# A graph network on one core: the segment mask as loaded bytes, and the sum of messages on TensorE

## The reference

```python
h = (x @ W).reshape(n, H, C)
# loops are added: every node is its own neighbour too
e = leaky_relu(a_src[src] + a_dst[dst], 0.2)
e = exp(e - segment_max(e, dst)[dst])
alpha = e / (segment_sum(e, dst)[dst] + 1e-16)
msg = h[src] * alpha[:, :, None]
out = segment_sum(msg, dst) + bias
f = gelu(out)
f = (f - mean(f)) / sqrt(var(f) + 1e-5) * gamma + beta
return f + x
```

## Time and profile before

| | us |
|---|---|
| median of three runs | 3763.0 (3749.06 to 3767.47) |
| the profiled execution | 3756.52 |
| its span, first to last instruction | 3754.8 |
| VectorE busy | 3277.5 (87%) |
| TensorE busy | 2538.7 (68%) |
| ScalarE busy | 2505.5 (67%) |
| GpSimd busy | 2442.9 (65%) |
| mean granted TensorE clock | 0.782 of full |

### The profile page before, as it was taken

One profiled execution on the slowest core, in us unless ns is written; L12 is line 12 of the kernel. 1 busy time (PEld: TensorE's weight loads), 2 busy tenths in 40 slices (PEclk: granted clock), 3 DMA queues, 4 the chain that ended last, 5 costly groups with the idle time before them and its releaser, 6 DMA issues. The chain is left out here.

```text
span 3754.8 us, 45520 instructions
## 1 busy us (share of the span) xinstructions
PE 2538.7 (68%) x10538; PEld 1633.2 (43%) x10538; DVE 3277.5 (87%) x7566; ACT 2505.5 (67%) x5570; POOL 2442.9 (65%) x2202
## 2 busy tenths in 40 slices
PE   5888888888724444267567567658788885777774
PEld 3555555555401222166566556524444442444442
DVE  5999999999877999699789789869999996998886
ACT  3888888888832666556546557747777774665554
POOL 4666666666614666477677677667666633787777
PEclk9999999999966777576676677679998986665555
DMA  3888877777647999578778678623333323333331
GB/s 104 203 223 207 212 216 210 217 212 216 199 122 210 268 271 272 172 227 275 226 227 277 214 229 257 194 80 95 87 85 84 85 69 85 89 98 92 97 96 58
DMA packets 421065, 643.89 MB, mean 171 GB/s; under 512 B 128031, under 2 KB 226728, under 8 KB 420798
## 3 DMA queue, kind: packets, MB, share of 16 engines
q1 hardware_dynamic: 351038, 527.96, 46.8%
q0 software_dynamic: 69760, 113.02, 12.7%
HBM read 347.78 MB, written 296.81 MB: 172 GB/s over the span
## 5 line engine op out<-in xcount | busy, mean ns | idle before, releaser
L915 POOL DMA_INDIRECT gs_t<-table_x,slot_idx x392 | 439.5, 1121 | 310.8 <-POOLq L87 126.1
L1651 POOL DMA_INDIRECT gs_g<-table_h,slot_idx x392 | 417.7, 1066 | 158.4 <-issue 115.8
L522 POOL DMA_INDIRECT gs<-x,src_idx x200 | 220.6, 1103 | 261.3 <-DMA xd_rows<-gd 150.6
L1290 POOL DMA_INDIRECT slot_idx<-node_map,src_idx x200 | 250.7, 1253 | 192.0 <-DMA slot_idx<-node_map,src_idx 95.8
L385 PE MATMUL ps<-ident,gs_g 128*128 128x128 f32 x588 | 131.7, 366 | 264.0 <-DMA gs_g<-table_h,slot_idx 156.7
L1702 ACT ACTIVATE h_e_g<-zb_g,inv 128x128 f32<-128x128 f32 x392 | 124.9, 390 | 249.6 <-DVE zb_g L1785 249.6
L2008 POOL DMA_INDIRECT out<-x_t,end_idx x196 | 234.4, 1196 | 60.3 <-issue 59.7
L1651 POOL DMA_INDIRECT gs_g<-table_x,slot_idx x196 | 208.1, 1062 | 96.4 <-issue 94.9
L522 POOL DMA_INDIRECT gd<-x,dst_idx x200 | 223.3, 1116 | 60.9 <-issue 60.0
L915 POOL DMA_INDIRECT own_t<-table_x,own_idx x196 | 221.4, 1129 | 59.7 <-issue 59.7
L1770 DVE TENSOR_TENSOR_SCAN agg_g<-same_seg,agg_g,ps 128x512 f32<-128x512 uint8 x147 | 187.3, 1274 | 83.3 <-PE ps L385 83.2
(11 more groups left out here) (378 smaller groups left out, 9015.5 us busy)
## 6 DMA issues: line engine op xcount, KB each, us to landing
table_x<-x_b SPq DMA_DIRECT2D x99, 512.0 KB
table_h<-h_b SPq DMA_DIRECT2D x98, 512.0 KB
x_in<-x SPq DMA_DIRECT2D x49, 512.0 KB
table_h<-h_e_g SPq DMA_DIRECT2D x98, 256.0 KB
own_g<-table_h SPq DMA_DIRECT2D x98, 256.0 KB, 4.7
pen_t<-pen_row SPq DMA_DIRECT2D x98, 256.0 KB, 3.8
table_x<-x_b SPq DMA_DIRECT2D x48, 384.0 KB
y_g<-table_x SPq DMA_DIRECT2D x48, 384.0 KB, 6.2
```

Of the source, the lines that this page charges most:

```text
L522: pool.indirect_dma_start(out=to[k % 3][:, j * D:(j + 1) * D], out_offset=None, in_=x, in_offset=bass.IndirectOffsetOnAxis(ap=of[:, n:n + ...
L915: pool.indirect_dma_start(out=self.B[L % RING][g][:, t * D:(t + 1) * D], out_offset=None, in_=table, in_offset=bass.IndirectOffsetOnAxis(a ...
L1290: pool.indirect_dma_start(out=slot_idx[:, t:t + 1], out_offset=None, in_=node_map, in_offset=bass.IndirectOffsetOnAxis(ap=src_idx[:, t:t + ...
L1651: pool.indirect_dma_start(out=gs[c % 6][:, j * D:(j + 1) * D], out_offset=None, in_=tables[layer], in_offset=bass.IndirectOffsetOnAxis(ap= ...
```

## The change

- Preparation: VectorE copies the mask to bytes (`same_u8`), and SyncE stores it as `same_row`.
- Softmax part: SyncE loads `same_row` once, broadcast to 128 partitions, into `same_seg`; it waits for the landing at the end of the part.
- Stage 3: the loads of `nst` and ScalarE's casts are gone; the scan reads its mask from `same_seg`.
- Stage 3: `with_self` is gone from VectorE. TensorE multiplies the identity with the message total and with the own message, accumulating both in `T_D2` (signal `o_ps`), and Gelu reads `T_D2`. The own product of the next pair, which writes the same bank, waits for Gelu instead of the own message. In TensorE's order the four products stand between the source products and the own products. `as_b` is free for its next load after `o_ps`.

```diff
@@ -94,6 +94,7 @@
     nst_row = dram("nst_row", [1, ET])
     nxt_row = dram("nxt_row", [1, ET])
     cnt_row, own_row = dram("cnt_row", [1, ET]), dram("own_row", [1, ET])
+    same_row = dram("same_row", [1, ET], U8)
     z8, a8 = dram("z8", [8, ET]), dram("a8", [8, ET])
     xsT_d, xdT_d = dram("xsT_d", [P, ET]), dram("xdT_d", [P, ET])
     xd_rows = dram("xd_rows", [ET, D])
@@ -154,6 +155,7 @@
         edge_i = tb("edge_i", [H, 2, 4, P], I32)
         edge_f = tb("edge_f", [H, 2, 4, P])
         mark = tb("mark", [H, 2, 5, P])
+        same_u8 = tb("same_u8", [H, 2, P], U8)
         att = tb("att", [P, 2, D])
         prod = tb("prod", [P, 4, D])
         sums = tb("sums", [P, 6, 4])
@@ -202,7 +204,9 @@
                 sp.wait_ge(S("marks"), 2)
                 for row, k in ((nst_row, 1), (pen_row, 2), (nxt_row, 0)):
                     sp.dma_start(row.rearrange("o (h r c) -> (o r) h c", h=2, c=P), mark[:, :, k, :]).then_inc(S("rows_stored"), 16)
-                sp.wait_ge(S("rows_stored"), 48)
+                sp.wait_ge(S("same_u8"), 1)
+                sp.dma_start(same_row.rearrange("o (h r c) -> (o r) h c", h=2, c=P), same_u8[:]).then_inc(S("rows_stored"), 16)
+                sp.wait_ge(S("rows_stored"), 64)
                 sp.wait_ge(S("stored"), 32)
 
             @block.gpsimd
@@ -274,6 +278,7 @@
                 v.wait_ge(S("m"), 3)
                 V.tensor_tensor(mark[:, :, 3, :], mark[:, :, 4, :], edge_f[:, :, 1, :], ALU.add).then_inc(S("marks"), 1)
 
+                V.tensor_copy(same_u8[:], mark[:, :, 1, :]).then_inc(S("same_u8"), 1)
                 v.wait_ge(S("masks"), 5)
                 V.tensor_scalar(centre[:], ident[:], 1.0 / D, None, ALU.subtract).then_inc(S("centre"), 1)
                 v.wait_ge(S("win_ps"), 1)
@@ -1040,6 +1045,7 @@
                     sp.dma_start(nxt[h * SECT:(h + 1) * SECT, :], sections(nxt_row)).then_inc(S("masks_in"), 16)
                 sp.dma_start(z[:], sections(z8[0:4, :])).then_inc(S("z_in"), 16)
                 sp.dma_start(zs[:], sections(z8[4:8, :])).then_inc(S("zs_in"), 16)
+                sp.dma_start(same_seg[:], same_row.to_broadcast([P, ET])).then_inc(S("same_seg"), 16)
                 sp.wait_ge(S("cnt_fix"), 1)
                 sp.dma_start(sections(cnt_row), cnt[0:SECT, :]).then_inc(S("cnt_out"), 16)
                 sp.wait_ge(S("cnt_out"), 16)
@@ -1053,6 +1059,7 @@
                 sp.wait_ge(S("a_self"), 1)
                 sp.dma_start(sections(a8[4:8, :]), zs[:]).then_inc(S("a_out"), 16)
                 sp.wait_ge(S("a_out"), 32)
+                sp.wait_ge(S("same_seg"), 16)
                 sp.wait_ge(S("deg4_in"), 16)
 
             @block.gpsimd
@@ -1214,7 +1221,7 @@
         def ring(name, n, shape=(P, 2 * CH)):
             return [tmp.enter_context(nc.sbuf_tensor(f"{name}_h{k}", list(shape), F32)) for k in range(n)]
 
-        xsT, xdT, a_b, as_b, nst = (ring(n, 2) for n in ("xsT", "xdT", "a_b", "as_b", "nst"))
+        xsT, xdT, a_b, as_b = (ring(n, 2) for n in ("xsT", "xdT", "a_b", "as_b"))
         xd, x1_b, num, t_b, xs_b = ring("xd", 3), ring("x1_b", 3), ring("num", 2), ring("t_b", 2), ring("xs_b", 3)
         n_b = ring("n_b", 1)[0]
         gT = ring("gT", 2, (P, CH))
@@ -1263,16 +1270,13 @@
                         for h in range(4):
                             sp.dma_start(a_b[c % 2][32 * h:32 * h + 32, :], pair_cols(a8[h:h + 1, :], c).to_broadcast([32, W2])).then_inc(S(f"a_in{c % 2}"), 16)
                         if c >= 2:
-                            sp.wait_ge(S("same_seg"), c - 1)
-                        sp.dma_start(nst[c % 2][:], pair_cols(nst_row, c).to_broadcast([P, W2])).then_inc(S(f"nst_in{c % 2}"), 16)
-                        if c >= 2:
                             sp.wait_ge(S("hd_ps"), 2 * (c - 1))
                         sp.dma_start(xdT[c % 2][:], pair_cols(xdT_d, c)).then_inc(S(f"xdT_in{c % 2}"), 16)
                         if c >= 3:
                             sp.wait_ge(S("w"), 2 * (c - 2))
                         sp.dma_start(by_half(xd[c % 3][:]), pair_rows(xd_rows, c, 0)).then_inc(S(f"xd_in{c % 3}"), 16)
                         if c >= 2:
-                            sp.wait_ge(S("gelu"), 2 * (c - 1))
+                            sp.wait_ge(S("o_ps"), 2 * (c - 1))
                         for h in range(4):
                             sp.dma_start(as_b[c % 2][32 * h:32 * h + 32, :], pair_cols(a8[4 + h:5 + h, :], c).to_broadcast([32, W2])).then_inc(S(f"as_in{c % 2}"), 16)
                     if live(t - 2):
@@ -1309,13 +1313,20 @@
                     if h == 0:
                         landed(pe, "xdT_in", 2, n)
                     if n:
-                        pe.wait_ge(S("self_msg"), 2 * n - 1 + h)
+                        pe.wait_ge(S("gelu"), 2 * n - 1 + h)
                     nc.tensor.matmul(T_D2[h], W0[:], half(xdT[n % 2], h), start=True, stop=True).then_inc(S("hd_ps"), 1)
 
                 for t in range(-1, N_P):
                     n = t + 1
                     if live(n):
                         source_products(n)
+                    if live(t):
+                        pe.wait_ge(S("num"), t + 1)
+                        for h in range(2):
+                            pe.wait_ge(S("self_msg"), 2 * t + h + 1)
+                            nc.tensor.matmul(T_D2[h], ident[:], half(num[t % 2], h), start=True, stop=False)
+                            nc.tensor.matmul(T_D2[h], ident[:], half(as_b[t % 2], h), start=False, stop=True).then_inc(S("o_ps"), 1)
+                    if live(n):
                         own_product(n, 0)
                         own_product(n, 1)
                     for h in range(2):
@@ -1342,15 +1353,12 @@
                 for t in range(N_P + 4):
                     r, b = rs[t % 2], nm[t % 2]
                     c = t - 3
-                    if live(t):
-                        landed(act, "nst_in", 2, t)
-                        nc.scalar.copy(same_seg[:, t * W2:(t + 1) * W2], nst[t % 2][:]).then_inc(S("same_seg"), 1)
                     for h in range(2):
                         if live(t):
-                            act.wait_ge(S("o"), 2 * t + h + 1)
+                            act.wait_ge(S("o_ps"), 2 * t + h + 1)
                             if t:
                                 act.wait_ge(S("g_ps"), 2 * t - 1 + h)
-                            nc.scalar.activation(gT[h][:], half(as_b[t % 2], h), ACT.Gelu, bias=bias0_col[:, 0:1]).then_inc(S("gelu"), 1)
+                            nc.scalar.activation(gT[h][:], T_D2[h], ACT.Gelu, bias=bias0_col[:, 0:1]).then_inc(S("gelu"), 1)
                     act.wait_ge(S("scaled"), t + 1)
                     for h in range(2):
                         if live(t - 1):
@@ -1389,11 +1397,6 @@
                     v.wait_ge(S(f"as_in{t % 2}"), 64 * (t // 2 + 1))
                     V.tensor_tensor(half(as_b[t % 2], h), T_D2[h], half(as_b[t % 2], h), ALU.mult).then_inc(S("self_msg"), 1)
 
-                def with_self(t, h):
-                    v.wait_ge(S("num"), t + 1)
-                    v.wait_ge(S("self_msg"), 2 * t + h + 1)
-                    V.tensor_tensor(half(as_b[t % 2], h), half(num[t % 2], h), half(as_b[t % 2], h), ALU.add).then_inc(S("o"), 1)
-
                 def residual(q, h):
                     if h == 0:
                         landed(v, "xd_in", 3, q)
@@ -1416,13 +1419,12 @@
                         for h in range(2):
                             v.wait_ge(S("hs_ps"), 2 * t + h + 1)
                             V.tensor_tensor(half(a_b[t % 2], h), T_S[h], half(a_b[t % 2], h), ALU.mult).then_inc(S("msg"), 1)
-                        landed(v, "nst_in", 2, t)
                         v.wait_ge(S("msg"), 2 * t + 2)
                         if t:
                             v.wait_ge(S("num"), t)
                         if t >= 2:
-                            v.wait_ge(S("o"), 2 * (t - 1))
-                        V.tensor_tensor_scan(num[t % 2][:], nst[t % 2][:], a_b[t % 2][:], num[(t - 1) % 2][:, W2 - 1:W2], ALU.mult, ALU.add).then_inc(S("num"), 1)
+                            v.wait_ge(S("o_ps"), 2 * (t - 1))
+                        V.tensor_tensor_scan(num[t % 2][:], same_seg[:, t * W2:(t + 1) * W2], a_b[t % 2][:], num[(t - 1) % 2][:, W2 - 1:W2], ALU.mult, ALU.add).then_inc(S("num"), 1)
                     if live(t - 1):
                         v.wait_ge(S("a_st"), 4 * t)
                     if live(t - 2):
@@ -1435,12 +1437,9 @@
                     v.wait_ge(S("batch"), n0 + 1)
                     V.tensor_scalar(shifted[:], big.bitcast(I32)[:], 1, None, ALU.logical_shift_right).then_inc(S("batch"), 1)
                     if live(t):
-                        with_self(t, 0)
                         self_message(t, 1)
                     v.wait_ge(S("batch"), n0 + 2)
                     V.tensor_scalar(half_y[:].bitcast(I32), shifted[:], -1.0, float(MAGIC), ALU.mult, ALU.add).then_inc(S("batch"), 1)
-                    if live(t):
```

(1 more changed line is left out.)

## The result

The changed kernel takes 3774.6 us (median of 20 runs, 3763.5 to 3782.1) against 3760.5 for the kernel before on the same chips (20 runs): a ratio of 1.0036, 95% interval 1.0027 to 1.0045, some 14 us slower. The forecast was +37 us and a range of 3768 to 3824: the time lies inside the range, and the change goes the way that was forecast, but it is little more than a third of the size. The prediction took 19 us as the least that can be told from no change; over 20 runs of each kernel the interval is narrower, and it leaves out 1.

A forecast was written before the change was run, and what follows sets the result against it. VectorE's program order was taken to set the stage's pass, with transfers full but not late. 23 passes x 1.57 us, +2 for the last pass and -1 for the fill gave +37 on 3763: 3800 us, range 3768 to 3824.

The forecast's parts named there:

- What bounds the stage, and the chain: Stage 3: VectorE's order sets the 15.53 us pass; after the change, TensorE's sums and own products delay transposes and statistics.
- The statistics' wait: Sign in stage 3: VectorE's row statistics wait about 3 us, up to 4, in every pass for TensorE's transposes.
- The n_b waits: Sign in stage 3: VectorE's waits for ScalarE's normalised rows, 0.24 and 0.70 us a pass, are gone.
- The DMA share: Sign in stage 3: the DMA engines' busy share, 91% before, falls below 0.85.
- The pass at the full clock: Stage 3 pass with TensorE at its upper clock: 16.24 us against 15.53, +0.71 us a pass.
- The clock's share: Stage 3 sums at TensorE's lower clock until a rise 5.5 us into the burst: +0.86 us a pass.
- Fill and drain: Stage 3's ends: -1 us while it fills (between -4 and 0), +2 us for cold sums in the last pass.
- The clock rival: TensorE's clock stays up, or rises early in every burst of stage 3: +13 us, about 3776; chance 0.15.
- The faster rival: Stage 3: VectorE's saved 1.38 us a pass come home, 34 us in all, 3729; chance 0.08.
- The mask load: Softmax part: one 3.3 MB load takes 13 us, costs 0; a slow-load rival adds some 26 us, 3826, chance 0.06.

The follow-up runs named there:

- e7_before_warm: Kernel before plus five useless TensorE products a pass after the transposes, to raise its clock; ratio 0.9998 to before.
- e6_one_product: Changed kernel with the message total left out of the sums, two products less a pass (a probe with an incomplete result); ratio 0.9913 to before.
- e3_own_last: Changed kernel with the next pair's two own products moved behind the transposes in TensorE's order; ratio 0.9972 to before.
- e4_warm: Changed kernel plus five useless products on TensorE after each pair's transposes, filling its gap to keep the clock up; ratio 1.0000 to before.
- the mask part alone: Kernel before with only the byte mask, its f32 mask loads and casts gone from stage 3, additions still on VectorE; ratio 0.9969 to before.
- e8_half: Changed kernel with half 1's sum back on VectorE and TensorE reordered: source products, sum 0, own product 1, transposes, own product 0; 3731.0 us, ratio 0.9920.
- e5_own_last_warm: Changed kernel with own products behind the transposes and five useless TensorE products a pass filling the gap; ratio 0.9952 to before.

## Why the prediction was wrong in size

- **What bounds the stage, and the chain.** Right. VectorE's order set the pass (e7_before_warm: a TensorE clock of 0.83 instead of 0.73 changes nothing), and after the change the chain from the sums to the statistics does (e6_one_product, e3_own_last). The statistics' wait was forecast at 3 to 4 us and is 2.54 to 3.71. The n_b waits went, as said. The passes were to be about 17 us apart and are 16.19. The DMA share is 0.76 from 1200 to 1500 us, below the 0.85 named.
- **The pass at the full clock.** Forecast 16.24 us, +0.71; measured 15.61 to 15.62 (e4_warm), +0.1. This is the term that failed most. No step is missing, but each was sized high. Forecast and measured, from the pass shown above: the sums start at 4.56 and 4.45; the own products at 8.20 and 7.96; the transposes at 10.18 and 9.87; the statistics at 10.97 and 10.54; the gamma multiply at 12.40 and 11.88; the next pass at 16.24 and 15.61. Seven hundredths to 0.13 us in each of six segments make 0.63 us, on a term of 0.71. Most of it is how rows were read. Each sum was priced at 0.91 us, half of what two products took until the next work began, with the lead-in of the first one in it; the four took 0.88 us each (0.13 in all). The 0.79 us from the transposes to the statistics came from a burst of the earlier trace rows whose transposes began at 1175.56 at the lower clock (the two rows below, of the kernel before, have it rise between 1175.75 and 1176.00); at the full clock it is 0.67 (0.12).

```profile
1175.50:1175.75 0.25, 0.25 (x2) 0.50 1.40 247
1175.75:1176.00 0.25, 0.25 (x4) 0.78 0.66 148
```

The lengths of rows were also added up where instructions that wait for nothing overlap a little: from the statistics to the gamma multiply 1.42 us were counted and 1.34 passed, and the two gamma multiplies, 0.69 each when each waited, take 1.27 together (1315.24). In the Gelu segment 8.36 + 0.72 is 9.08 and not 9.12. The own message was simply 0.11 earlier than before; why is open. The term was the small difference of two long chains, and the forecast gave no spread for that: its lower end of 0.7 a pass stood for the clock alone. (The same 0.79 us would have given the chain before 1.7 us to spare, and not the 1.2 that the prediction read from the end of the transposes; the sum does not use it.)

- **The clock's share.** The mechanism and its price were right: 0.49 us for each us of the sums at the lower clock fits all four kinds of pass within 0.05. The choice of a late rise, 5.5 us in every burst, was wrong: the rises come at 2.9, 4.3, 5.4 and 6.0 in turn, mean 4.65, close to the mean of 4.6 that the rows of before gave. The mean cost is 0.57, not 0.86. The remark that rises and bursts influence each other was right in that the passes fall into a rhythm; but the rhythm goes through all delays, and does not stay at a late one.
- **Together** the passes were forecast at 23 x 1.57 = 36.1 us and gave 23 x 0.66 = 15.2, of which 0.57 a pass is the clock and 0.1 the chain at the full clock.
- **Fill and drain.** -1 and +2 were forecast, -1.7 and +2.2 measured. The -1 hides two larger terms, though, which the runs took apart: -7.3 for the mask part alone, more than the 4 us that were set as its bound, and about +4 to +5.6 for the sums on top of it (e4_warm and the changed kernel).
- **The clock rival** forecast 3776, and 3774.6 was measured. Its mechanism did not happen: the clock fell in every gap shown. The time agrees only because the full-clock pass was forecast 0.6 us too long, about what the clock costs.
- **The faster rival** asked for the transposes 7.95 us into the pass; the statistics waited 2.54 to 3.71 us for them. Much of what it priced at 34 us can be had by another way: e8_half has 21.5 us of it in the stage, 4.5 of them in the fill.
- **The mask load** of the softmax part delayed nothing: it landed 12.4 us after its issue (13 were forecast), and from the first load of the softmax part to that of stage 3 it takes 53.6 us in both kernels (1095.74 to 1149.32 before, 1093.28 to 1146.92 after).

What stays open: the 20 runs of the changed kernel spread from 3763.5 to 3782.1, and the profiled one is at their low end. Whether other executions fall into another rhythm of clock and passes can't be said from one profile. That the fill's gain is 7.3 us rather than the 4 us of two loads is seen in the two waits, but it was not taken apart further. Nor is it shown why the part after the stage differs by up to 28 us between executions of the same code.

## What to carry to other kernels

Moving work from the fullest engine to an idle one helps only if it lands in the idle engine's gap. Here the sums stood ahead of the transposes for which the full engine was waiting, with two products that nobody needed yet in between; moving these two behind the transposes turned 1.0036 into 0.9972, and leaving half of the work where it was, with the rest in an order to match, gave 0.9920. When the forecast is a small difference of two long chains, put the reading error of every segment into the range, and measure the parts of a change alone: here one part was a gain that the other ate up. Take a price from a row whose clock is known, and from start to start of what follows, not from the length of the row.

## What the runs showed of the hardware

TensorE's clock and a loop that depends on it can fall into a rhythm: with the sums on the path the passes were 15.61, 15.95, 16.50 and 16.78 us over and over, in e3_own_last 14.83 and 15.88 in turn, and in e6_one_product 14.1 with one of about 15 every four or five. In the changed kernel each comes from where in the burst the clock rises, 2.9 to 6.0 us after its start, and in both orders the spread went when the gap was filled (e4_warm, e5_own_last_warm); for e6_one_product this was not tried. A single pass read from such a trace can be off by 1.2 us.
